# A graph layer on 32 batches: row scales transposed one unit later, VectorE's loop turned at another point of its period, and a new order at the start

## The chip, the cores and the metric

The kernel runs on one core of one Trainium2 chip. The metric is the device time of one execution in microseconds (us); the engines are TensorE (PE), VectorE (DVE), ScalarE (ACT), POOL (GpSimd) and SP (SyncE, which here only issues transfers).

## The reference

The input `x` has 32 batches of 512 channels and 1024 nodes in float32. Per batch:

```
h = relu(layernorm(x over nodes))
q, k = wq.h, wk.h
scores = q[None, :] + k[:, None];  scores = leaky_relu(scores, 0.01)
att = softmax(scores over the last axis)
agg[c, m] = sum_n h[c, n] att[m, n]
out = relu(adj @ agg + bm)
x + out
```

`adj` (512 x 512) serves as the weight matrix of the layer; `wq`, `wk` and `bm` have 512 elements.

## The kernel before

Batches go in pairs, named (i, j) with j 0 or 1; `nxt(b, n)` is the batch n further on, `first` and `second` are (0, 0) and (0, 1). The order of each engine's work is written out by hand, and semaphores tie the engines together. Each float32 operand of a matrix product is split into an upper and a lower float16 part (`h_hi`/`h_lo`, `v_hi`/`v_lo`, `p_hi`/`p_lo`), and three products of parts are summed.

For every batch there are these pieces of work:

- **Normalising.** VectorE takes statistics of `xs` (L633) and computes scale and shift (normaliser). ScalarE writes `h_hi` (L458) and the full `h` in float32 (L464) into one of two buffers; VectorE subtracts them to `h_lo` (h_lower, L687; for the first batch L676).
- **v phase** on TensorE: project_qk (L321) computes q and k, select_qk (L330) brings them into columns after VectorE's copy `qk_rows` (q_rows, L696), spread_qmax (L336) transposes the maximum for VectorE's q_tail. Between them stand eight v_tile of 12 matmuls each (L356 to L358). ScalarE and VectorE split each tile (v_upper L492, v_lower L757).
- **Softmax.** Since the scores are a sum of a row and a column under a leaky relu, the exponential of each is the maximum of two products of a row and a column vector. VectorE sums the rows (denominator, L724, 16 per batch) and turns the sums into row scales `ab_pad` (row_scales, L731 to L735). TensorE transposes `ab_pad` (transpose_ab, L343), VectorE copies the result to `ab_t` (copy_ab, L681), SP writes it to DRAM (L242) and reads it back, spread over the partitions, as `ab_row` (L248).
- **Weights p.** For each of 16 steps per batch ScalarE writes `p_ring` (leak, L480), VectorE takes the maximum (weight, L745), ScalarE writes `p_hi` (L488), VectorE `p_lo` (p_lower, L752). There are two halves of 8 steps; half_0 of a batch is computed one period ahead, the second half in the period itself.
- **Units.** In period b TensorE computes 8 units of 24 matmuls (L379 to L381) from `v` and `p` of b: units 0 to 3 on the first half of p, units 4 to 7 on the second. ScalarE applies the relu (L499), POOL adds `x` (L876), SP stores.

TensorE's period b is: 8 units of b, with transpose_ab(nxt(b)) between them, then the v phase of nxt(b, 2). VectorE's period b is: the second half of the weights of b, between them the denominators of nxt(b); row_scales; h_lower of nxt(b, 2) 0 and 1; copy_ab; h_lower 2 and 3; half_0 of nxt(b); then v_lower, q_head, q_tail, statistics and normaliser of the v phase that TensorE runs meanwhile. The two periods of a pair are the body of a hardware loop: 13 rounds on VectorE and SP, 14 on TensorE, ScalarE and POOL. The periods before and behind are written out.

At the start SP loads the first batch, ScalarE's queue the weights. Absolute sums of the weights give power-of-two scales (scaled_weights on VectorE), POOL scales the weights (L870), TensorE transposes them (L306), and `wmT_hi`/`wmT_lo` come from ScalarE (L450) and VectorE (L622).

Of the kernel before, what the change touches and what calls it, by code (L numbers as in the profile page):

```python
# [43 lines left out]
def gnn_layer(nc, x, adj, wq, wk, bm, out):  # L44
# [14 lines left out]
    with ExitStack() as ctx:  # L59
# [86 lines left out]
        s_su = sem("scaling_chain")  # L146
        s_wqk = sem("wqk_ready")
# [6 lines left out]
        s_h32 = sem("h32_ready")  # L154
        s_hlo = sem("h_split")
# [144 lines left out]
        def _(pe):  # L300
# [44 lines left out]
            def v_tile(b, nt):  # L345
# [55 lines left out]
            pe.wait_ge(s_wqk, 3)  # L401
            project_qk(first)
            select_qk(first)
            spread_qmax(first)
            pe.wait_ge(s_wl, CT)
            for nt in range(NT):
                v_tile(first, nt)
            project_qk(second)
            for nt in range(NT):
# [4 lines left out]
                if nt == 4:  # L414
                    transpose_ab(first)
# [11 lines left out]
        def _(act):  # L427
# [38 lines left out]

            def exponentials(b):
# [27 lines left out]
            def relu(b, k):  # L495
                hf, ot = divmod(k, OT)
                act.wait_ge(s_acc, cnt(b, U, k + 1))
# [51 lines left out]
            h_full(first, 2)  # L549
            weights_upper()  # L550
            h_full(first, 3)
# [31 lines left out]
        def _(dve):  # L583
            def scaled_weights():
                n = [0]

                def link(ins):
                    n[0] += 1
                    ins.then_inc(s_su, 1)
                    dve.wait_ge(s_su, n[0])  # L590

                dve.wait_ge(s_abs, OT + 2)
                dve.wait_ge(s_wv, 16 * 3)

                link(dve.tensor_scalar(rows[:, :], rows[:, :], 1e-25, 1e30, ALU.max, ALU.min))
                link(dve.tensor_scalar(pow2[:, :].bitcast(I32), rows[:, :].bitcast(I32), 0x7F800000, None,
                                       ALU.bitwise_and))
                link(dve.reciprocal(inv2[:, :], pow2[:, :]))
# [3 lines left out]
                dve.tensor_scalar(unscale_o[:, :], pow2[:, 0:OT], 1.0 / (V_BITS * P_SCALE), None,  # L602
                                  ALU.mult).then_inc(s_su, 1)
                dve.tensor_scalar(unscale_q[:, :], pow2[:, OT:OT + 2], 1.0 / (Q_BITS * H_SCALE), None,
                                  ALU.mult).then_inc(s_su, 1)
                n[0] += 4
                dve.wait_ge(s_su, n[0])
                link(dve.memset(wqk[:, :, :], 0.0))
                hi = wqk[:, :, 0:4].rearrange("p t (i s) -> p s i t", s=2)
                link(dve.tensor_copy(hi[:, 0], wqk_col[:, :, :]))  # L610
                dve.tensor_tensor(hi[:, 1], wqk_col[:, :, :], hi[:, 0], ALU.subtract).then_inc(s_wqk, 1)
                dve.wait_ge(s_id, 2)
                pairs = ident[:, :].rearrange("p (g j) -> p g j", g=NQ)[:, :, 0:4].rearrange("p g (i s) -> p s g i", s=2)
                link(dve.tensor_tensor(select[:, :, :], pairs[:, 0], pairs[:, 1], ALU.add))
                for i in range(2):
                    dve.tensor_scalar(select[:, :, i], select[:, :, i], unscale_q[:, i:i + 1], None,
                                      ALU.mult).then_inc(s_wqk, 1)

            def weights_lower():
                for ct in range(CT):  # L620
                    dve.wait_ge(s_wh, ct + 1)
                    dve.tensor_tensor(wmT_lo[:, ct, :], wmT_ps[ct][:, :], wmT_hi[:, ct, :],  # L622
                                      ALU.subtract).then_inc(s_wl, 1)
# [42 lines left out]
            def h_full_first(ct):  # L666
                dve.wait_ge(s_ln, LN_OPS)
                wait(dve, s_hlo, ct - 1)
                dve.tensor_scalar(h32[:, ct % 2, :], xs[:, ct, :], ln_scale[:, 0, ct:ct + 1],
                                  ln_shift[:, 0, ct:ct + 1], ALU.mult, ALU.add).then_inc(s_h32, 1)  # L670

            def h_lower_first(ct):

                dve.wait_ge(s_hhi, ct + 1)
                dve.wait_ge(s_h32, ct + 1)
                dve.scalar_tensor_tensor(out=h_lo[:, 0, ct, :], in0=h32[:, ct % 2, :], scalar=0.0,  # L676
# [91 lines left out]
            def period(b, one, two, three):  # L768
# [45 lines left out]
            for ct in range(CT):  # L814
# [96 lines left out]
```

## Time and profile before

| | before |
|---|---|
| median of 3 runs | 2242.95 us (2241.51 to 2243.74) |
| the profiled execution's own time | 2246.45 us |
| its span | 2244.7 us |
| TensorE busy | 2090.1 us, 93% |
| VectorE busy | 1677.6 us, 75% |
| ScalarE busy | 1225.5 us, 55% |
| POOL busy | 367.9 us, 16% |
| mean granted TensorE clock | 0.973 of full speed |
| DMA | 271.46 MB |

The span is the time from the first to the last instruction of one profiled execution. A wait is idle time of an engine, put down to what released it; "issue" is idle time in which the profile shows nothing that the engine waited for. The starts and ends of matmuls overlap, as they are pipelined: from one start to the next counts.

### The profile page before, as it was taken

How to read it: one execution, taken by the hardware profiler on the slowest of the kernel's cores; microseconds unless marked ns; L12 is line 12 of the kernel's file. 1: busy time of each engine (PE TensorE's matmuls, PEld its weight loads, DVE VectorE, ACT ScalarE, POOL GpSimd, SP SyncE). 2: the span in 40 equal slices, each digit the busy share in tenths (PEclk: the TensorE clock that was granted, in tenths of full speed). 3: DMA queues.
4: the chain of work that ended last, by engine and by line, in shares of the span. 5: the costliest groups of instructions: out<-in, count | busy, mean ns of one | idle time of the engine just before them, and what ended most of it. 6: DMA issues, size and time to landing. Idle time of an engine off the chain costs nothing.

```text
span 2244.7 us, 33555 instructions
## 1 busy us (share of the span) xinstructions
PE 2090.1 (93%) x10448; PEld 956.9 (43%) x10448; DVE 1677.6 (75%) x3667; ACT 1225.5 (55%) x1871; POOL 367.9 (16%) x267
## 2 busy tenths in 40 slices
PE   5899998998989989899898998989989899899999
PEld 2344443443434434444343444434434344344444
DVE  7977787767877678786787767777677777778853
ACT  4655664545645456464565545655456655456634
POOL 0011211111211112111121111211112111122112
PEclk8999999999999999999999999999999999999999
DMA  5134342333323333233442234332343323434222
GB/s 187 70 129 151 132 135 73 125 136 131 141 77 115 136 131 144 83 114 128 136 145 91 102 127 150 131 110 92 122 145 131 127 82 115 145 131 150 89 90 85
DMA packets 126395, 271.46 MB, mean 121 GB/s; under 512 B 22624, under 2 KB 23136, under 8 KB 122208
## 3 DMA queue, kind: packets, MB, share of 16 engines
q1 hardware_dynamic: 123904, 269.01, 34.6%
q10 hardware_dynamic: 2400, 1.58, 0.2%
q14 instruction: 76, 0.62, 0.1%
q8 instruction: 15, 0.25, 0.0%
HBM read 202.91 MB, written 67.63 MB: 121 GB/s over the span
## 4 chain that ended last, share of the span: by engine, by line
PE 56%; DVE 27%; issue 14%; ACT 1%; DMA 1%; DVEq 0%; POOLq 0%; SPq 0%; ACTq 0%
DVE den_out L724 9%; PE mix L379 9%; PE mix L380 9%; PE mix L381 9%; PE mix L356 9%; PE mix L358 8%; PE mix L357 8%; DVE p_ring L745 6%; DVE p_lo L752 5%; PE small L321 1%; DVE den L731 1%; ACT v_hi L492 1%; DVE rstd L659 1%; DVE t_y L658 1%; DVE half_y L656 1%
## 5 line engine op out<-in xcount | busy, mean ns | idle before, releaser
L379 PE MATMUL mix<-p_hi,v_hi 128*128 128x512 f16 x2048 | 789.4, 385 | 5.1 <-DVE p_lo L752 4.4
L380 PE MATMUL mix<-p_lo,v_hi 128*128 128x512 f16 x2048 | 788.1, 385 | 0.0
L381 PE MATMUL mix<-p_hi,v_lo 128*128 128x512 f16 x2048 | 787.2, 384 | 0.0
L876 POOL TENSOR_TENSOR res<-res,y 128x512 f32<-128x512 f32 x256 | 364.3, 1423 | 1856.2 <-ACT y L499 1856.2
L745 DVE SCALAR_TENSOR_TENSOR p_ring<-ab_row,cols,p_ring 128x512 f32<-128x512 f32 x512 | 376.0, 746 | 188.7 <-ACT p_ring L480 131.1
L480 ACT ACTIVATE p_ring<-ab_row,cols 128x512 f32<-128x512 f32 x512 | 349.4, 691 | 166.9 <-DMA ab_row<-ab_rows 106.5
L492 ACT ACTIVATE v_hi<-mix 128x512 f16<-128x512 f32 x256 | 152.7, 597 | 522.6 <-PE mix L358 522.6
L724 DVE SCALAR_TENSOR_TENSOR den_out<-den_row,cols 128x512 f32<-128x512 f32 x512 | 392.4, 802 | 0.0
L356 PE MATMUL mix<-wmT_hi,h_hi 128*128 128x512 f16 x1024 | 389.6, 380 | 0.0
L357 PE MATMUL mix<-wmT_lo,h_hi 128*128 128x512 f16 x1024 | 389.1, 380 | 0.0
L358 PE MATMUL mix<-wmT_hi,h_lo 128*128 128x512 f16 x1024 | 389.1, 380 | 0.0
L757 DVE SCALAR_TENSOR_TENSOR v_lo<-mix,v_hi 128x512 f16<-128x512 f32 x256 | 176.8, 691 | 269.2 <-ACT v_hi L492 266.5
L488 ACT ACTIVATE p_hi<-p_ring 128x512 f16<-128x512 f32 x512 | 302.7, 591 | 124.3 <-DVE p_ring L745 124.3
L752 DVE SCALAR_TENSOR_TENSOR p_lo<-p_ring,p_hi 128x512 f16<-128x512 f32 x512 | 350.3, 684 | 22.5 <-ACT p_hi L488 18.1
L379 PEld LDWEIGHTS mix<-p_hi,v_hi 128*128 128x128 f16 x2048 | 203.1, 99 | 253.4 <-issue 13.9
L381 PEld LDWEIGHTS mix<-p_hi,v_lo 128*128 128x128 f16 x2048 | 203.0, 99 | 249.8 <-issue 14.5
L380 PEld LDWEIGHTS mix<-p_lo,v_hi 128*128 128x128 f16 x2048 | 203.2, 99 | 244.7 <-issue 12.0
L499 ACT ACTIVATE y<-mix,bias_o,unscale_o 128x512 f32<-128x512 f32 x256 | 196.0, 765 | 73.2 <-PE mix L381 73.1
L464 ACT ACTIVATE h<-xs,ln_shift,ln_scale 128x1024 f32<-128x1024 f32 x122 | 147.5, 1232 | 108.8 <-DVE h_lo L687 107.2
L633 DVE BATCH_NORM_STATS2 stats<-xs 128x6 f32<-128x512 f32 x248 | 158.2, 680 | 8.5 <-DMA xs<-in_x_dram 8.5
L356 PEld LDWEIGHTS mix<-wmT_hi,h_hi 128*128 128x128 f16 x1024 | 102.9, 101 | 119.4 <-issue 7.7
L358 PEld LDWEIGHTS mix<-wmT_hi,h_lo 128*128 128x128 f16 x1024 | 100.4, 98 | 121.7 <-issue 1.4
(69 smaller groups left out, 834.1 us busy)
## 6 DMA issues: line engine op xcount, KB each, us to landing
res<-in_x_dram SPq DMA_DIRECT2D x256, 256.0 KB, 2.9
out_dram<-res SPq DMA_DIRECT2D x256, 256.0 KB, 2.1
xs<-in_x_dram SPq DMA_DIRECT2D x124, 512.0 KB, 6.5
den_row<-den_rows SPq DMA_DIRECT2D x32, 1024.0 KB, 4.6
ab_row<-ab_rows SPq DMA_DIRECT2D x64, 512.0 KB, 4.7
res<-in_x_dram SPq DMA_DIRECT2D x4, 512.0 KB, 5.2
wm_nat<-in_adj_dram ACTq DMA_DIRECT2D x1, 1024.0 KB, 12.2
den_rows<-cols SPq DMA_DIRECT2D x32, 8.0 KB, 1.6
```

The costliest lines, as they stand in the source:

```text
L356: pe.matmul(ps[:, :], hi, wmT_hi[:, ct, :], start=(ct == 0), stop=False)
L357: pe.matmul(ps[:, :], hi, wmT_lo[:, ct, :], start=False, stop=False)
L358: mm = pe.matmul(ps[:, :], lo, wmT_hi[:, ct, :], start=False, stop=(ct == CT - 1))
L379: pe.matmul(ps[:, :], v_hi[:, b[1], nt, chans], p_hi[:, hf, nt, :], start=(nt == 0), stop=False)
L380: pe.matmul(ps[:, :], v_hi[:, b[1], nt, chans], p_lo[:, hf, nt, :], start=False, stop=False)
L381: mm = pe.matmul(ps[:, :], v_lo[:, b[1], nt, chans], p_hi[:, hf, nt, :], start=False, stop=(nt == NT - 1))
L480: act.activation(ring[t % RING][:, :], ab_row[:, 1, hf * HALF:(hf + 1) * HALF], ACT.Copy, scale=cols[:, b[1], 1, nt:nt + 1]).then_inc(s_lk, 1)
L488: act.activation(p_hi[:, hf, nt, :], ring[t % RING][:, :], ACT.Copy, scale=P_SCALE).then_inc(s_phi, 1)
L724: dve.scalar_tensor_tensor(out=den_out[:, nodes], in0=den_row[:, 0, nodes], scalar=cols[:, b[1], 2, nt:nt + 1], in1=den_row[:, 1, nodes], ...
L745: dve.scalar_tensor_tensor(out=ring[t % RING][:, :], in0=ab_row[:, 0, hf * HALF:(hf + 1) * HALF], scalar=cols[:, b[1], 0, nt:nt + 1], in1= ...
L752: dve.scalar_tensor_tensor(out=p_lo[:, hf, nt, :], in0=ring[t % RING][:, :], scalar=P_SCALE, in1=p_hi[:, hf, nt, :], op0=ALU.mult, op1=ALU ...
L876: pool.tensor_tensor(res[:, k, :], res[:, k, :], y[:, k % 2, :], ALU.add).then_inc(s_add, 1)
```

## The change

In the steady periods two things change. transpose_ab(nxt(b)) moves on TensorE from unit 4, before its fifth group of three matmuls, to unit 5, before its third group. On VectorE the period is cut into early(b), up to h_lower(h, 3), and late(b), from half_0 on; the loop's body is now late, early, late, early, so that it turns between the last h_lower and half_0, and the first early of the loop is written out ahead of it. The order of VectorE's instructions is the same, and so is the number of rounds.

At the start: the scaling chain is split. POOL clears `wqk` and computes `select`, `unscale_q` and `unscale_o`. The first batch's full `h` of channels 2 and 3 goes into `ab_row` and no longer waits for a buffer of two. VectorE places `scaled_wqk` between the `h_lo` of the first batch, its weights_lower around q_rows, two of the second batch's statistics ahead of q_tail and its normaliser ahead of the `v_lo`. On TensorE spread_qmax(first) stands behind the first v tile, which waits for each `wmT_lo` by itself; the first transpose_ab stands one tile earlier.

```diff
@@ TensorE, v_tile, unit, start @@
                 for ct in range(CT):
+                    if nt == 0 and at(b, first):
+                        pe.wait_ge(s_wl, ct + 1)
...
                 for nt in range(NT):
-                    if one and k == MIX and nt == 4:
+                    if one and k == MIX + 1 and nt == 2:
                         transpose_ab(nxt(b))
...
             transposed_weights()
-            pe.wait_ge(s_wqk, 3)
+            pe.wait_ge(s_wqk, 1)
             project_qk(first)
+            pe.wait_ge(s_sel, 3)
             select_qk(first)
-            spread_qmax(first)
-            pe.wait_ge(s_wl, CT)
             for nt in range(NT):
+                if nt == 1:
+                    spread_qmax(first)
                 v_tile(first, nt)
...
-                if nt == 4:
+                if nt == 3:
                     transpose_ab(first)
@@ ScalarE @@
+            def h_full_first(ct):
+                act.activation(ab_row[:, ct - 2, :], xs[:, ct, :], ACT.Relu, bias=ln_shift[:, 0, ct:ct + 1],
+                               scale=ln_scale[:, 0, ct:ct + 1]).then_inc(s_h32f, 1)
...
-            h_full(first, 2)
+            h_full_first(2)
+            h_full_first(3)
             weights_upper()
-            h_full(first, 3)
             exponentials(first)
@@ VectorE: scaled_weights is split @@
-            def scaled_weights():
...
+            def weight_scales():
...
+            def scaled_wqk():
...
+            def weights_lower(ct):
+                dve.wait_ge(s_wh, ct + 1)
+                dve.tensor_tensor(wmT_lo[:, ct, :], wmT_ps[ct][:, :], wmT_hi[:, ct, :],
+                                  ALU.subtract).then_inc(s_wl, 1)
...
-            def period(b, one, two, three):
+            def early(b, one, two):
                 h = nxt(b, 2)
                 weight(b, NT)
...
                     h_lower(h, 2)
                     h_lower(h, 3)
+
+            def late(b, one, two, three):
+                h = nxt(b, 2)
                 if one:
                     half_0(nxt(b))
...
@@ VectorE, start @@
-            scaled_weights()
-            for ct in range(CT):
-                h_lower_first(ct)
+            weight_scales()
+            h_lower_first(0)
+            h_lower_first(1)
+            scaled_wqk()
+            h_lower_first(2)
+            h_lower_first(3)
+            weights_lower(0)
+            weights_lower(1)
             q_rows(first)
-            weights_lower()
+            weights_lower(2)
+            weights_lower(3)
             q_head(first)
+            statistics(second, 0)
+            statistics(second, 1)
             q_tail(first)
-            for ct in range(CT):
-                statistics(second, ct)
+            statistics(second, 2)
+            statistics(second, 3)
+            normaliser(second)
             v_lower(first, 0)
-            normaliser(second)
             v_lower(first, 1)
+            v_lower(first, 2)
             denominator(first, 0)
-            v_lower(first, 2)
-            denominator(first, 1)
             for ct in range(CT):
                 h_lower(second, ct)
                 v_lower(first, 3 + ct)
-                denominator(first, 2 + ct)
+                denominator(first, 1 + ct)
             v_lower(first, 7)
             q_rows(second)
+            denominator(first, 5)
             denominator(first, 6)
             q_head(second)
             denominator(first, 7)
             row_scales(first)
+            q_tail(second)
             v_lower(second, 0)
-            q_tail(second)
@@ VectorE, the periods @@
-            period((0, 0), True, True, True)
-            period((0, 1), True, True, True)
+            early((0, 0), True, True)
+            late((0, 0), True, True, True)
+            early((0, 1), True, True)
+            late((0, 1), True, True, True)
+            early((1, 0), True, True)
             with dve.Fori(1, PAIRS - 1) as i:
-                period((i, 0), True, True, True)
-                period((i, 1), True, True, True)
+                late((i, 0), True, True, True)
+                early((i, 1), True, True)
+                late((i, 1), True, True, True)
+                early((i + 1, 0), True, True)
...
@@ POOL, start @@
+            pool.memset(wqk[:, :, :], 0.0).then_inc(s_wz, 1)
             pool.memset(ab_pad[:, :], 0.0).then_inc(s_az, 1)
...
+            pool.wait_ge(s_id, 2)
...
+            pool.tensor_scalar(unscale_q[:, :], pow2[:, OT:OT + 2], 1.0 / (Q_BITS * H_SCALE), None,
+                               ALU.mult).then_inc(s_un, 1)
+            pool.tensor_tensor(select[:, :, :], pairs[:, 0], pairs[:, 1], ALU.add).then_inc(s_sel, 1)
+            pool.wait_ge(s_un, 1)
+            pool.wait_ge(s_sel, 1)
+            for i in range(2):
+                pool.tensor_scalar(select[:, :, i], select[:, :, i], unscale_q[:, i:i + 1], None,
+                                   ALU.mult).then_inc(s_sel, 1)
+            pool.tensor_scalar(unscale_o[:, :], pow2[:, 0:OT], 1.0 / (V_BITS * P_SCALE), None,
+                               ALU.mult).then_inc(s_un, 1)
```

VectorE's rows at the end of the loop's body, before (the branch is the turn; the row behind it is the first after the last round):

```order
L662 SCALAR_TENSOR_TENSOR ln_shift<-moments,rstd 128x4
L756 REGISTER_ALU
L757 SCALAR_TENSOR_TENSOR v_lo<-mix,v_hi 128x512
L852 REGISTER_ALU
L852 COMPARE_AND_BRANCH
L745 SCALAR_TENSOR_TENSOR p_ring<-ab_row,cols,p_ring 128x512 x2
```

And with the change:

```order
L691 TENSOR_TENSOR h_lo<-h,h_hi 128x1024
L685 COPY ab_t<-small 16x128
L689 REGISTER_ALU
L691 TENSOR_TENSOR h_lo<-h,h_hi 128x1024
L689 REGISTER_ALU
L691 TENSOR_TENSOR h_lo<-h,h_hi 128x1024
L870 REGISTER_ALU
L870 COMPARE_AND_BRANCH
L749 SCALAR_TENSOR_TENSOR p_ring<-ab_row,cols,p_ring 128x512 x2
L756 SCALAR_TENSOR_TENSOR p_lo<-p_ring,p_hi 128x512
```

The branch stood behind the last `v_lo` of a period; it now stands behind the last two `h_lo`, ahead of the `p_ring` of half_0.

TensorE's rows around the transpose of the row scales in a steady period, before:

```order
L379 MATMUL mix<-p_hi,v_hi 128x512
L380 MATMUL mix<-p_lo,v_hi 128x512
L381 MATMUL mix<-p_hi,v_lo 128x512
L343 MATMUL small<-ident,ab_pad 128x128
L379 MATMUL mix<-p_hi,v_hi 128x512
L380 MATMUL mix<-p_lo,v_hi 128x512
```

And with the change:

```order
L385 MATMUL mix<-p_hi,v_hi 128x512
L386 MATMUL mix<-p_lo,v_hi 128x512
L387 MATMUL mix<-p_hi,v_lo 128x512
L347 MATMUL small<-ident,ab_pad 128x128
L385 MATMUL mix<-p_hi,v_hi 128x512
L386 MATMUL mix<-p_lo,v_hi 128x512
```

In the program the transpose stood at row 323 of TensorE's stream and stands now at row 341: 18 matmuls later.

## Rows read from the trace of the kernel before

**Rows 1.** TensorE's waits over the whole span: engine, tile, line <- who ended it: us in total, times, longest

```profile
PE small L343 <- DVE ab_pad L735: 116.6, 31, 7.0
```

**Rows 2.** TensorE's waits from 350 to 2045 us

```profile
PE small L343 <- DVE ab_pad L735: 103.3, 24, 7.0
```

**Rows 3.** Line 343 by stretches: count, ns min/median/max, first and last start; below, who released it

```profile
L343 PE MATMUL small<-ident,ab_pad x1: 327/327/327, 114.6 to 114.6; 128*128 128x128 f32 x1
  DVE ab_pad L735: 3.9, 1
...
L343 PE MATMUL small<-ident,ab_pad x1: 329/329/329, 249.8 to 249.8; 128*128 128x128 f32 x1
...
L343 PE MATMUL small<-ident,ab_pad x1: 329/329/329, 2180.1 to 2180.1; 128*128 128x128 f32 x1
```

**Rows 4.** Timeline of TensorE: start us, us, engine, line, operation [idle before <- releaser]

```profile
315.70 0.33 PE L343 MATMUL small<-ident,ab_pad 128*128 128x128 f32 x1 [1.86 <-DVE ab_pad L735]
...
386.62 0.47 PE L343 MATMUL small<-ident,ab_pad 128*128 128x128 f32 x1 [6.88 <-DVE ab_pad L735]
...
391.71 0.38 PE L379 MATMUL mix<-p_hi,v_hi 128*128 128x512 f16 x1
...
393.65 0.38 PE L379 MATMUL mix<-p_hi,v_hi 128*128 128x512 f16 x1
```

**Rows 5.** Timeline of VectorE where its loop turns

```profile
363.69 1.42 DVE L745 SCALAR_TENSOR_TENSOR p_ring<-ab_row,cols,p_ring 128x512 f32<-128x512 f32 x2 [4.93 <-issue]
```

**Rows 6.** VectorE's waits over the whole span

```profile
DVE p_ring L745 <- issue: 57.6, 12, 5.0
```

**Rows 7.** The chain that ended last, about 340 and 358 us: start us, us, what

```profile
340.43 0.34 PE small L330 x4
...
358.24 3.06 issue
361.45 2.23 issue
```

**Rows 8.** Stretches: us, busy us of the engines (instructions), granted clock, DMA share, GB/s

```profile
320.00:330.00 10.00, 10.00 (x48) 4.53 (x47) 5.27 (x9) 5.59 (x10) 2.97 (x2) 1.00 0.95 317
...
321.00:331.00 10.00, 10.00 (x48) 4.50 (x47) 5.67 (x9) 6.59 (x12) 2.00 (x2) 1.00 1.02 356
359.00:363.00 4.00, 4.00 (x21) 1.80 (x19) 0.00 (x0) 0.00 (x0) 0.00 (x0) 1.00 0.01 4
...
386.50:391.50 5.00, 4.88 (x13) 1.87 (x14) 4.92 (x6) 2.37 (x2) 0.00 (x0) 0.51 0.29 107
```

**Rows 9.** Timeline of VectorE in an undisturbed period

```profile
313.98 0.68 DVE L752 SCALAR_TENSOR_TENSOR p_lo<-p_ring,p_hi 128x512 f16<-128x512 f32 x1
...
315.47 0.17 DVE L735 TENSOR_TENSOR ab_pad<-cols,ab_pad 128x8 f32<-128x8 f32 x1
...
317.92 0.27 DVE L681 COPY ab_t<-small 16x128 f32<-16x128 f32 x1
...
324.84 1.42 DVE L745 SCALAR_TENSOR_TENSOR p_ring<-ab_row,cols,p_ring 128x512 f32<-128x512 f32 x2 [4.24 <-ACT p_ring L480]
...
335.87 0.41 DVE L696 COPY qk_rows<-small 128x256 f32<-128x256 f32 x1
```

**Rows 10.** Waits of SP, which issues the transfers

```profile
SPq L237 <- DMA den_rows<-cols: 40.4, 32, 4.4
```

**Rows 11.** Timeline of TensorE at the start

```profile
28.76 0.41 PE L321 MATMUL small<-h_hi,wqk 128*32 128x256 f16 x4 [5.58 <-DVE h_lo L676]
...
34.18 0.63 PE L356 MATMUL mix<-wmT_hi,h_hi 128*128 128x512 f16 x1
...
92.36 0.38 PE L379 MATMUL mix<-p_hi,v_hi 128*128 128x512 f16 x1
```

**Rows 12.** Timeline of VectorE at the start

```profile
43.63 0.16 DVE L662 SCALAR_TENSOR_TENSOR ln_shift<-moments,rstd 128x4 f32<-128x4 f32 x1
...
78.30 1.41 DVE L745 SCALAR_TENSOR_TENSOR p_ring<-ab_row,cols,p_ring 128x512 f32<-128x512 f32 x2 [1.11 <-ACT p_ring L480]
```

More of the change, by code:

```diff
@@ L146, in gnn_layer @@
         s_su = sem("scaling_chain")
+        s_wz = sem("wqk_zeroed")
+        s_un = sem("unscales_ready")
+        s_sel = sem("select_ready")
         s_wqk = sem("wqk_ready")
@@ L154, in gnn_layer @@
         s_h32 = sem("h32_ready")
+        s_h32f = sem("first_h32_upper_channels")
         s_hlo = sem("h_split")
@@ L496, in relu @@
                 hf, ot = divmod(k, OT)
+                if k == 0 and at(b, first):
+                    act.wait_ge(s_un, 2)
                 act.wait_ge(s_acc, cnt(b, U, k + 1))
@@ L601, in scaled_weights @@
                                       ALU.mult, ALU.mult).then_inc(s_su, 1)
[L602 to L608, printed above, removed]
+                dve.wait_ge(s_su, 5)
+                dve.wait_ge(s_wz, 1)
                 hi = wqk[:, :, 0:4].rearrange("p t (i s) -> p s i t", s=2)
-                link(dve.tensor_copy(hi[:, 0], wqk_col[:, :, :]))
+                dve.tensor_copy(hi[:, 0], wqk_col[:, :, :]).then_inc(s_su, 1)
+                dve.wait_ge(s_su, 6)
                 dve.tensor_tensor(hi[:, 1], wqk_col[:, :, :], hi[:, 0], ALU.subtract).then_inc(s_wqk, 1)
[L612 to L619, printed above, removed]
-                for ct in range(CT):
-                    dve.wait_ge(s_wh, ct + 1)
-                    dve.tensor_tensor(wmT_lo[:, ct, :], wmT_ps[ct][:, :], wmT_hi[:, ct, :],
-                                      ALU.subtract).then_inc(s_wl, 1)
+            def weights_lower(ct):
+                dve.wait_ge(s_wh, ct + 1)
+                dve.tensor_tensor(wmT_lo[:, ct, :], wmT_ps[ct][:, :], wmT_hi[:, ct, :],
+                                  ALU.subtract).then_inc(s_wl, 1)
             def statistics(b, ct):
@@ L667, in h_full_first @@
                 dve.wait_ge(s_ln, LN_OPS)
-                wait(dve, s_hlo, ct - 1)
-                dve.tensor_scalar(h32[:, ct % 2, :], xs[:, ct, :], ln_scale[:, 0, ct:ct + 1],
-                                  ln_shift[:, 0, ct:ct + 1], ALU.mult, ALU.add).then_inc(s_h32, 1)
+                dve.tensor_scalar(h32[:, ct, :], xs[:, ct, :], ln_scale[:, 0, ct:ct + 1],
+                                  ln_shift[:, 0, ct:ct + 1], ALU.mult, ALU.add).then_inc(s_h32, 2)
             def h_lower_first(ct):
                 dve.wait_ge(s_hhi, ct + 1)
-                dve.wait_ge(s_h32, ct + 1)
-                dve.scalar_tensor_tensor(out=h_lo[:, 0, ct, :], in0=h32[:, ct % 2, :], scalar=0.0,
+                if ct < 2:
+                    src = h32[:, ct, :]
+                    dve.wait_ge(s_h32, 2 * (ct + 1))
+                else:
+                    src = ab_row[:, ct - 2, :]
+                    dve.wait_ge(s_h32f, ct - 1)
+                dve.scalar_tensor_tensor(out=h_lo[:, 0, ct, :], in0=src, scalar=0.0,
                                          in1=h_hi[:, 0, ct, :], op0=ALU.max, op1=ALU.subtract).then_inc(s_hlo, 1)
@@ L849, in _ @@
                     v_lower(second, 4 + nt // 2)
-            period((0, 0), True, True, True)
-            period((0, 1), True, True, True)
-            with dve.Fori(1, PAIRS - 1) as i:
-                period((i, 0), True, True, True)
-                period((i, 1), True, True, True)
-            period((PAIRS - 1, 0), True, True, True)
-            period((PAIRS - 1, 1), True, True, False)
-            period((PAIRS, 0), True, False, False)
-            period((PAIRS, 1), False, False, False)
+            early((0, 0), True, True)
[3 more added lines that the diff above has]
+            early((1, 0), True, True)
+            with dve.Fori(1, PAIRS - 1) as i:
+                late((i, 0), True, True, True)
+                early((i, 1), True, True)
+                late((i, 1), True, True, True)
+                early((i + 1, 0), True, True)
+            late((PAIRS - 1, 0), True, True, True)
+            early((PAIRS - 1, 1), True, True)
+            late((PAIRS - 1, 1), True, True, False)
+            early((PAIRS, 0), True, False)
+            late((PAIRS, 0), True, False, False)
+            early((PAIRS, 1), False, False)
         @block.gpsimd
```

18 lines of the change are left out of this document (8 added, 10 removed).

## The prediction, made before the changed kernel had run

> **What bounds the kernel now.** I read the page first: TensorE is busy 93% of the span and VectorE 75%, so the question is what stands in TensorE's other 7%. The list of TensorE's waits answers it: 116.6 us in 31 waits of one instruction, the small transpose L343 of the row scales, for VectorE's `ab_pad` L735 [rows 1]. Then the single waits. There are two kinds: 1.86 us in an undisturbed period (at 315.70) and 6.88 us after VectorE's loop has turned (at 386.62) [rows 4]. The same list for 350 to 2045 us has 24 of them, 103.3 us [rows 2]: 12 of each kind.
>
> Where the long ones come from, VectorE's timeline shows: an instruction at 363.69 stands after 4.93 us of idleness in which nothing was waited for, "issue" [rows 5]. That happens 12 times, 57.6 us [rows 6], as often as a loop of 13 rounds turns back, between the last `v_lo` of a period and the first `p_ring` of the next. From there VectorE runs without a gap up to `ab_pad` 23 us later, so the whole turn reaches TensorE (6.88 - 1.86 = 5.0).
>
> A second loss follows: after the long wait the granted clock is 0.51 for 5 us, the level of 1.2 GHz, against 1.00 (2.4 GHz) before and after [rows 8]. I price it by periods, from transpose to transpose. The clean one is 249.8 to 315.70 = 65.9, less 1.86 = **64.04 us** of work. From 114.6 to 2180.1 are 30 periods and 2065.5 us [rows 3]; 30 x 64.04 = 1921.2, so 144.3 are lost. The waits in them are 116.6 less the first, 3.9: 112.7. The other **31.6 us** are the clock, mostly 2.4 for each of 12 turns.
>
> **Term 1, the transpose one unit later.** It moves from unit 4, tile 4, to unit 5, tile 2: 18 matmuls of 0.2155 us (9 of them from 391.71 to 393.65 [rows 4]) = 3.88 us later. In the undisturbed period TensorE was ready at 315.70 − 1.86 = 313.84, so now at 317.72; `ab_pad` is done at 315.64 [rows 4, 9]. The wait is gone with 2.1 us to spare. What is late next? The unit's last tile needs the last `p_lo`, done at 314.66 (313.98 + 0.68); TensorE reaches it 9 matmuls after 313.84, at 315.78: 1.1 us to spare. Behind the transpose VectorE copies its result at 317.92, after two `h_lo`; now the result is there at 317.72 + 0.33 = 318.05, so the copy, the two row DMAs of SP queued behind it and the first `p_ring` slip by some 0.2 us. VectorE idles 4.24 us before that `p_ring` [rows 9], and TensorE needs those weights only a v phase later. By itself this move would take the 12 long waits from 6.9 to 3 or 4.
>
> **Term 2, the turn of VectorE's loop moved** from the end of the v phase to between the last `h_lo` of early() and half_0. The row beside it is the gap of 4.24 us before `p_ring` at 324.84, a wait for ScalarE, which waits for the row DMAs. The gap begins at 320.60; plus 4.93 is 325.53, so the turn makes half_0 0.7 us late, with the copy 0.9. TensorE's first need of VectorE behind it is L330, which needs `qk_rows`, done at 335.87 + 0.41 = 336.28; L330 ran at 340.43, and with the 1.9 us that TensorE gains at 338.57 [rows 7, 9]. So VectorE may be 2.3 us late, and is 0.9: 1.4 us of cover. With that cover gone TensorE would stand at L330, and behind it the v phase. VectorE has short waits before its `v_lo` there, in which it catches up. Every wait of TensorE for `ab_pad` goes: 116.6, less what the first period keeps.
>
> The trace has no turn at the new place, so its length is bounded: below, 4.93 us less what VectorE's sequencer may run ahead (no loss at all); above, by the transfers. At the old place the DMA engines carry 4 GB/s during the turn at a share of 0.01 and nothing else; from 321 to 331 us, the new place, they are at 1.02 with 356 GB/s [rows 8]. Small transfers wait under load: the one before L237 takes 40.4 / 32 = 1.3 us, at worst 4.4 [rows 10]. The chain shows the turn in two pieces, 3.06 and 2.23 us [rows 7]. If each is a transfer of code, the turn grows by at most 2 × 3.1 = 6.2 us. The Trainium skill ("Runtime: NRT & Kernel Launch", section "Instruction fetch mechanics") speaks for that reading: a taken branch to code outside the window held forces a DMA fetch before the engine goes on. By that rule the turn is a transfer and suffers from the load (up to 58 us more in all); by the idle row alone it stays 4.93 and costs nothing. The trace agrees as far as the 4 GB/s go; no row shows a fetch under load. Between 0 and (6.2 − 1.4) × 12 = 58 us I take 0.3 per turn, **3.6 us**, near the lower end, since the branch can be reached while the last `h_lo` (1.2 us) still runs, and the burst only begins with it.
>
> **Term 3, the clock.** With no wait left it has no idleness to fall after: in 320 to 330 TensorE is busy 10.00 of 10 us at 1.00 [rows 8]. The 31.6 us come back.
>
> **Term 4, the start.** The first projection (28.76) waits 5.58 us for `h_lo` [rows 11], because ScalarE's third `h` waits for a buffer and the fourth comes after the weights. Now both follow the `h_hi` directly, in `ab_row`: `h_lo` ends about 25.1, 3.5 us earlier, and v_tile 0 starts near 28.6 instead of 34.18 [rows 11], as the spread of the maximum moves behind it. But the spread then comes 12 slow matmuls later at about 33.7, as before (it ran just ahead of 34.18): `q_tail`, the exponentials and the row DMAs don't move. What moves is the second batch's normaliser: two of its four statistics now stand ahead of `q_tail`, and a `v_lo` behind it, so it ends at about 40.5 instead of 43.8 [rows 12], 3.3 earlier. Behind it VectorE works nearly without gaps up to the copy of the scales, and the row DMAs follow that; so the first `p_ring` comes at about 75.1 instead of 78.30 [rows 12]. Unit 0 of the first batch is tied to `p_lo`, so it ends **3.2 us** earlier. The scaling chain's parts now on POOL (some 10 small operations, memset included) hide behind the projection, as `select` is wanted only near 27.6.
>
> In the first period the wait of 3.9 becomes one for the last `p_lo`: from the start of unit 1 (92.36 [rows 11]) TensorE needs 93 × 0.2155 = 20.0, at 112.4; it is done one us before `ab_pad` (the transpose is at 114.6 [rows 3]), at 113.5. So 1.1 stays and 115.5 of the 116.6 go.
>
> **Sum.** 115.5 + 31.6 + 3.2 − 3.6 = 146.7. The profiled execution took 2246.45 (span 2244.7, 1.75 around it), so 2099.75. The median of the three runs, 2242.95, is 3.5 lower: **2096.3 us**.
>
> **The rivals.**
> *The turn grows under the DMA load* (above). For: share 1.02 at the new place. Against: the branch can be reached while `h_lo` still runs. One piece delayed by 3.1: (3.1 − 1.4) × 12 = 20, **2113**; both by 3.1, with the clock falling again (2.4 each): 58 + 29 − 4, **2179**.
> *VectorE's p_lo takes the place of the scales.* Cover 1.1 us. If VectorE runs 2 us later against TensorE, 0.9 × 28 = 25: **2121**. Against it: the 22.9 us from `v_lo` to `ab_pad` hold nothing that the change touches.
> *The turn does not go under the gap* but adds to it (the engine sees the wait only after the turn, and the copy, row loads and turn lie in series): 4.9 late, (4.9 + 0.2 − 2.3) × 12 = 34 − 4: **2127**. Then the change does only its first half.
> *Slower than before*, one mechanism: each of the two pieces of a turn waits for the burst of transfers, 10 us long from 321 on. Gain lost = 12 × (growth − 1.4 + 2.4); it is 150 us, the whole gain, at a growth of 11.5 us. At 15 the time is 2092.7 + 192 = **2285**. For: nothing but the share above 1. Against: small transfers grew by 3.1 at most.
>
> **How the numbers follow.** Forecast 0.70; the turn grown 0.15, p_lo 0.05, in series 0.06, slower 0.02, anything else on the fast side 0.02. About 0.2% (4.5 us) is what a measurement here can tell from no change; only the slower rival and its neighbourhood come near. Faster 0.97, same 0.01, slower 0.02. Range: below, the turn costs nothing (2092.7) and the start gives twice its 3.2 and more, 2087; above, it takes in the first rival's first half, the second and third, 2135.
>
> **What would show it.** Right: L343's successor waits for nothing; the 12 "issue" gaps stand before the first `p_ring` of half_0 with the wait for ScalarE smaller there, or are partly hidden; periods of 64.0 us throughout; granted clock 1.00 from 120 us on. Wrong: a wait of L330's successor for `qk_rows` in every second period; gaps above 6.3 us at the turn; waits for `p_lo` in unit 4; a first `p_ring` not before 77 us.

## The result and the profile after

The changed kernel takes **2089.64 us** (median of 4 runs, 2088.49 to 2090.47), the kernel before beside it 2242.39 us (2241.51 to 2243.74): a ratio of 0.9318, 95% interval 0.9302 to 0.9334, so 6.8% or 152.8 us less. I had forecast 2096.3 with a range from 2087 to 2135. The profiled execution took 2090.47 us, its span is 2088.7.

The page of the changed kernel, its busy times, the granted clock by slices, and the chain that ended last by engine:

```profile
PE 2051.5 (98%) x10448; PEld 950.3 (45%) x10448; DVE 1674.8 (80%) x3661; ACT 1221.5 (58%) x1871; POOL 379.6 (18%) x273
...
PEclk9999999999999999999999999999999999999999
...
PE 95%; DVE 3%; DMA 1%; POOL 0%; issue 0%; ACT 0%; POOLq 0%; SPq 0%; DVEq 0%
```

TensorE is busy 98% of the span instead of 93%, and the chain lies on it for 95%; before, the same line read PE 56%, DVE 27%, issue 14%. TensorE's waits, the view of [rows 1]:

```profile
PE mix L310 <- POOL wm_nat L893: 23.2, 2, 21.9
PE mix L385 <- DVE p_lo L756: 5.4, 8, 1.1
PE small L325 <- DVE h_lo L691: 2.8, 1, 2.8
PE small L334 <- DVE qk_rows L700: 0.6, 1, 0.6
PE mix L385 <- DVE v_lo L761: 0.5, 1, 0.5
```

The row of 116.6 us is gone and nothing of its size stands in its place; all that is left lies ahead of 112 us. The transposes, now L347, one by one, as in [rows 3]:

```profile
L347 PE MATMUL small<-ident,ab_pad x1: 272/272/272, 176.9 to 176.9; 128*128 128x128 f32 x1
...
L347 PE MATMUL small<-ident,ab_pad x1: 272/272/272, 240.7 to 240.7; 128*128 128x128 f32 x1
...
L347 PE MATMUL small<-ident,ab_pad x1: 272/272/272, 304.6 to 304.6; 128*128 128x128 f32 x1
...
L347 PE MATMUL small<-ident,ab_pad x1: 273/273/273, 368.4 to 368.4; 128*128 128x128 f32 x1
...
L347 PE MATMUL small<-ident,ab_pad x1: 272/272/272, 2028.0 to 2028.0; 128*128 128x128 f32 x1
```

Every period is 63.83 us long ((2028.0 - 176.9) / 29), with a turn of VectorE's loop in it (304.6 to 368.4 and every second one after) or without. The clock, by stretches (the columns of [rows 8]):

```profile
119.00:2080.00 1961.00, 1961.00 (x9995) 908.44 (x9994) 1574.86 (x3422) 1156.91 (x1774) 360.47 (x250) 1.00 0.38 130
```

From 119 to 2080 us TensorE is busy throughout, and the granted clock is 1.00, the upper level.

Where did the turn go? VectorE's timeline in a period in which the loop turns, behind the last `h_lo`, and what it waits for over the whole span (its row "issue" of [rows 6] doesn't exist any more):

```profile
366.33 0.17 DVE L739 TENSOR_TENSOR ab_pad<-cols,ab_pad 128x8 f32<-128x8 f32 x1
366.50 2.36 DVE L691 TENSOR_TENSOR h_lo<-h,h_hi 128x1024 f16<-128x1024 f32 x2
368.78 0.27 DVE L685 COPY ab_t<-small 16x128 f32<-16x128 f32 x1
369.11 2.36 DVE L691 TENSOR_TENSOR h_lo<-h,h_hi 128x1024 f16<-128x1024 f32 x2
375.44 1.41 DVE L749 SCALAR_TENSOR_TENSOR p_ring<-ab_row,cols,p_ring 128x512 f32<-128x512 f32 x2 [3.97 <-ACT p_ring L491]
...
386.40 0.41 DVE L700 COPY qk_rows<-small 128x256 f32<-128x256 f32 x1
```

```profile
DVE p_ring L749 <- ACT p_ring L491: 129.7, 33, 7.0
```

The first `p_ring` comes 3.97 us after `h_lo`, released by ScalarE. In the 27 periods between the fifth and the last the gap is 3.7 to 4.3 us, in those with a turn no longer than in the others. The turn lies wholly under a wait that was there anyway; how long it is there, the gap doesn't tell (see "How long a turn is"). It costs nothing, and the copy isn't late either: the transpose ends at 368.68, the copy starts at 368.78. TensorE's L334 ran at 389.04, 2.2 us behind `qk_rows`.

### The profile page after: what moved, and what is told of

Read it like the earlier page. It is cut to its first block, busy times and chain, and to the rows that moved or that the text cites. A ratio compares the mean times of both kernels' runs of the same rounds, so it can differ in the third digit from the quotient of the medians.

```text
span 2088.7 us, 33534 instructions
## 1 busy us (share of the span) xinstructions
PE 2051.5 (98%) x10448; PEld 950.3 (45%) x10448; DVE 1674.8 (80%) x3661; ACT 1221.5 (58%) x1871; POOL 379.6 (18%) x273
## 4 chain that ended last, share of the span: by engine, by line
PE 95%; DVE 3%; DMA 1%; POOL 0%; issue 0%; ACT 0%; POOLq 0%; SPq 0%; DVEq 0%
PE mix L385 21%; PE mix L387 21%; PE mix L386 21%; PE mix L362 10%; PE mix L363 10%; PE mix L364 10%; PE small L325 2%; DVE den_out L728 1%; PE small L334 1%; DMA xs<-in_x_dram 0%; DVE p_ring L749 0%; DVE p_lo L756 0%; DVE v_lo L761 0%; POOL wm_nat L893 0%; DMA den_row<-den_rows 0%
## 5 line engine op out<-in xcount | busy, mean ns | idle before, releaser
L385 PE MATMUL mix<-p_hi,v_hi 128*128 128x512 f16 x2048 | 776.3, 379 | 5.9 <-DVE p_lo L756 5.4
L386 PE MATMUL mix<-p_lo,v_hi 128*128 128x512 f16 x2048 | 776.2, 379 | 0.0
L387 PE MATMUL mix<-p_hi,v_lo 128*128 128x512 f16 x2048 | 776.2, 379 | 0.0
L911 POOL TENSOR_TENSOR res<-res,y 128x512 f32<-128x512 f32 x256 | 370.5, 1447 | 1688.2 <-ACT y L512 1688.2
```

The source lines that it names most:

```text
L385: pe.matmul(ps[:, :], v_hi[:, b[1], nt, chans], p_hi[:, hf, nt, :], start=(nt == 0), stop=False)
L386: pe.matmul(ps[:, :], v_hi[:, b[1], nt, chans], p_lo[:, hf, nt, :], start=False, stop=False)
L387: mm = pe.matmul(ps[:, :], v_lo[:, b[1], nt, chans], p_hi[:, hf, nt, :], start=False, stop=(nt == NT - 1))
L911: pool.tensor_tensor(res[:, k, :], res[:, k, :], y[:, k % 2, :], ALU.add).then_inc(s_add, 1)
```

## The experiments

All ratios are against the kernel before, run on the same chip beside each.

### Four kernels that take the change apart

The transpose alone, on the kernel before:

```diff
-                    if one and k == MIX and nt == 4:
+                    if one and k == MIX + 1 and nt == 2:
                         transpose_ab(nxt(b))
```

> The kernel before with the transpose moved from unit 4 to unit 5 and nothing else. My sum: the 16 short waits (1.86 us) go, 30 us; the 12 waits behind a turn shrink from 6.9 to what is left for the last p_lo, 5.0 - 1.1 = 3.9 us, 36 us. If the clock still falls after 3.9 us of waiting, as it did once at 114.5, the result is 2242.4 - 66 = 2176; if it does not, 29 us more, 2147. The rival, that the move gives nearly all (the turn would then never have reached TensorE through anything but the transpose), says 2100 or less.

Measured: **2158.6 us**, 0.9624 (0.9608 to 0.9640). The turn alone, on the kernel before:

```diff
             with dve.Fori(1, PAIRS - 1) as i:
-                period((i, 0), True, True, True)
-                period((i, 1), True, True, True)
+                late((i, 0), True, True, True)
+                early((i, 1), True, True)
+                late((i, 1), True, True, True)
+                early((i + 1, 0), True, True)
```

> The kernel before with VectorE's loop cut between the last h_lo and half_0 and nothing else. My sum: 12 long waits become short ones, 12 x 5.0 = 60 us, and the clock's loss behind them goes, up to 29 us: 2242.4 - 60 = 2182 if waits of 1.9 us also let the clock fall, 2153 if they don't. 28 waits of 1.86 us for ab_pad stay. The rival (the turn lies in series with the wait for the row loads, or grows under their load) says 2190 to 2240, with idle time of VectorE marked issue or a longer wait before p_ring.

Measured: **2158.91 us**, 0.9623 (0.9607 to 0.9639). Both of these diffs together, with the start of the kernel before:

> Both steady moves with the start of before. My sum leaves the start 3.2 us: 2089.6 + 3.2 = 2093. If the start is worth more (as the time below my forecast would allow), up to 2096; if nothing, 2090. No wait for ab_pad behind the first period.

Measured: **2091.94 us**, 0.9325 (0.9309 to 0.9340). And the changed kernel with both undone, that is with its start alone:

> The start of the change with the steady periods of before. By my sum 2242.4 - 3.2 = 2239. If the start helps only where TensorE waits for nothing else later, the waits for ab_pad eat none of it, since all later work moves with it: the same 2239. Nothing gained would be 2242.

Measured: **2242.58 us**, 1.0002 (0.9992 to 1.0012), no difference.

Either half of the steady change is worth 85 us, and both together 152, 18 less than the sum of 170. So they are mostly two debts, but not wholly: the wait behind a turn, 6.75 us on average, is shortened by either, by 4.9 us with the turn moved and by 3.3 with the transpose moved, which is 1.4 us more than there is to take, 12 times. Their traces say which is which. TensorE's largest wait with the transpose alone:

```profile
PE mix L379 <- DVE p_lo L752: 47.2, 32, 2.6
```

and with the turn alone:

```profile
PE small L343 <- DVE ab_pad L735: 58.0, 30, 3.9
```

With the transpose alone the 16 short waits are gone, and the 12 turns have moved to the last two `p_lo` of unit 4: 47.2 less the 5.4 of the start are 3.5 for each turn, where I had 3.9. The clock lies between my two cases: a period with a turn is 69.3 us and one without 63.8, so 2.0 us beside the wait. Part of that is the clock: behind the second wait, from 372.14 us on, matmuls stand 0.43 us apart for 3 us instead of 0.2155, which is 1.5 of the 2.0. With the turn alone the periods are 65.9 us throughout, that is 63.83 + 1.86 + 0.2: the short waits stay, and after them the clock does not fall here:

```profile
379.40:384.40 5.00, 5.00 (x24) 2.34 (x25) 4.78 (x5) 3.04 (x3) 0.75 (x1) 1.00 0.35 113
```

So the expectation for the turn alone (2153, clock kept) is met but for 6 us, the 0.2 us of 30 periods that the wait row doesn't contain.

The start alone is a miss, and an instructive one. In its trace the wait for `ab_pad` is 103.4 us instead of 116.6, and yet the 30 periods from 109.6 to 2174.5 us take 2064.9 us, where the kernel before needs 2065.5 from 114.6 to 2180.1. So 13 us less of waiting gained these periods 0.6 us; the rest went into the clock. After a short wait, in the kernel before and then in this one:

```profile
594.50:599.50 5.00, 5.00 (x25) 2.29 (x25) 4.71 (x5) 3.04 (x3) 0.82 (x1) 1.00 0.32 114
```

```profile
584.90:589.90 5.00, 5.00 (x16) 1.97 (x17) 4.82 (x5) 2.79 (x3) 0.00 (x0) 0.66 0.32 108
```

The first stays at 1.00 after its 1.9 us, the second falls after its 2.1; here that happens after 9 of 13 such waits, while in the kernel before it happened once, after a wait of 1.90 at 182.2 us. That the length of the wait decides is likely by this, not shown. And where did the 13 us less waiting come from? Not from the start, but from the turn, which has another shape:

```profile
354.89 1.41 DVE L749 SCALAR_TENSOR_TENSOR p_ring<-ab_row,cols,p_ring 128x512 f32<-128x512 f32 x2 [2.54 <-issue]
...
357.10 0.75 DVE L728 SCALAR_TENSOR_TENSOR den_out<-den_row,cols 128x512 f32<-128x512 f32 x1 [0.80 <-issue]
```

It takes 2.54 + 0.80 us where the kernel before has 4.93 in one piece [rows 5], at the same place of the period. In the loop nothing but its position in VectorE's stream differs, by a few instructions. That called for a test of its own.

### How long a turn is

Here 64, 128 and 192 waits on a semaphore that is long reached are put at VectorE's very start in the kernel before. Nothing else changes.

```diff
+            for _ in range(64):
+                dve.wait_ge(s_id, 1)
             for ct in range(CT):
                 statistics(first, ct)
```

> The kernel before with 64 more waits on a long reached semaphore at VectorE's very start, where it idles for the first load anyway; they only push the loop 64 instructions down VectorE's stream. In the start-only kernel, whose loop stands a few instructions higher, the turn took 2.5 us before the first p_ring and 0.9 before the first den_out instead of 4.8 in one. If the turn is a reload of code in blocks, its length and where it is felt depend on where the loop stands to the blocks: another split or length here, between 0 and 5 us, and the wait for ab_pad follows it one to one. If the difference had another cause (what runs beside it), the turn stays 4.8 us and the time 2243.6.

> As p64 with 128 waits. Reload in blocks: again another split or length. Otherwise 4.8 us and 2243.6.

> As p64 with 192 waits. Reload in blocks: again another split or length; with 64, 128 and 192 at least one of the three differs from 4.8 us by over 1 us. Otherwise 4.8 us in all three and 2243.6.

Measured: **2214.61** (0.9870, 0.9842 to 0.9899), **2215.96** (0.9876, 0.9848 to 0.9905) and **2237.7 us** (0.9976, 0.9965 to 0.9987). The program grows by 32, 64 and 96 instructions by the page, as two waits go into one. VectorE's turns, for 64, 128 and 192:

```profile
DVE p_ring L745 <- issue: 31.1, 12, 2.7
```

```profile
DVE p_ring L745 <- issue: 30.1, 12, 2.8
```

```profile
DVE p_ring L745 <- issue: 29.8, 12, 2.7
```

2.5 to 2.6 us each instead of 4.8, in all three. And the trace shows the reloads themselves: one DMA queue carries packets marked "instruction", 8 KB each. Its row (packets, MB, share of 16 engines) over one turn, from 358.5 to 363.7 us in the kernel before and from 356.7 to 359.1 with 64 waits:

```profile
q14 instruction: 2, 0.02, 1.0%
```

```profile
q14 instruction: 1, 0.01, 1.2%
```

It is so in every turn: two packets, 2.4 to 2.9 us apart, in each of the 12 turns of the kernel before and one in each of the 36 of the padded kernels. In the start-only kernel one lies in the first gap and the next begins at 355.3, 1.0 us ahead of the second. So the reading of the turn as a reload of code in blocks holds: the kernel before stood where it took two reloads, and a few dozen instructions further one is enough. The Trainium skill ("Runtime: NRT & Kernel Launch", section "Instruction fetch mechanics") states the rule for a taken branch to code outside the held window; the 2.5 and 4.8 us are this case's, and no run shows where the blocks' borders lie. That the 192 waits gain only 6.5 us, where the others gain 28 to 30, goes with what was just met: the same turn, but short waits of 2.1 us instead of 1.9 and a granted clock of 0.973 over the span, against 0.988 and 0.983. Why the short wait is 0.2 us longer there, no run shows.

The same row settles how long the turn is in the changed kernel. Over 371.0 to 375.5 us, the gap with the turn in it:

```profile
q14 instruction: 1, 0.01, 1.3%
```

The packet begins at 371.4, as the last `h_lo` ends, and the next one follows at 375.8, behind the `p_ring`; in the other turns the two are 3.6 us apart or more, where the kernel before had 2.4 to 2.9. So the moved turn took one reload and not the two that its 4.93 us stood for. The 2.5 us that one reload takes without load would fit into the gap of 4.24; whether the load that sets in there made it longer, the gap hides.

The other half of the question is what the load at the new place does to a turn. This kernel is the changed one with the loop turned in the middle of half_0, where VectorE has no gap and the transfers run:

```diff
-            def half_0(b):
-                weight(b, 0)
-                for nt in range(NT):
+            def half_0(b, steps):
+                if steps[0] == 0:
+                    weight(b, 0)
+                for nt in steps:
...
+                if one:
+                    half_0(nxt(b), range(4))
+
             def late(b, one, two, three):
                 h = nxt(b, 2)
                 if one:
-                    half_0(nxt(b))
+                    half_0(nxt(b), range(4, NT))
```

> The changed kernel with VectorE's loop turned in the middle of half_0, between its steps 3 and 4, where VectorE has no gap and the DMA engines are loaded. This bares the length of a turn under load. If it stays 4.9 us, qk_rows is 4.9 us late against 2.2 us of cover (386.81 to 389.04), 2.7 x 12 = 32 us: 2122, or 2151 with the clock falling each time. If each of its two pieces takes 3.1 us longer, 8.9 x 12 = 107 us: 2197 to 2225. The trace shows the idle time as issue.

Measured: **2108.0 us** (2100.94 to 2113.34), 0.9386 (0.9371 to 0.9400). One turn, the load around it (share 1.01, 408 GB/s), and the sums for VectorE and TensorE:

```profile
383.93 0.76 DVE L749 SCALAR_TENSOR_TENSOR p_ring<-ab_row,cols,p_ring 128x512 f32<-128x512 f32 x1 [2.91 <-issue]
...
513.59 0.76 DVE L749 SCALAR_TENSOR_TENSOR p_ring<-ab_row,cols,p_ring 128x512 f32<-128x512 f32 x1 [4.23 <-issue]
```

```profile
379.00:381.00 2.00, 2.00 (x11) 0.92 (x10) 2.00 (x4) 2.00 (x4) 0.00 (x0) 1.00 1.01 408
```

```profile
DVE p_ring L749 <- issue: 44.2, 12, 4.9
```

```profile
PE small L334 <- DVE qk_rows L700: 15.7, 13, 2.3
```

Turns under load last from 2.9 to 4.9 us, 3.7 on average, and they scatter, which the runs do too (12 us between the fastest and the slowest). Each of the 12 has one instruction packet in its gap, so the load adds 0.4 to 2.4 us to the 2.5 of one reload. It adds them before the packet: that begins 0.8 to 2.9 us after VectorE falls idle, 0.4 to 0.7 in the padded kernels. A turn of two reloads under load was not run; the rival of the prediction, growth to 11 us or more, had no sign of itself here. The price is near the sum: 3.7 less 2.2 of cover is 1.5 for a turn, 18 us, and by the medians 18.4 were measured. That the two are so close is luck: the turns are those of the profiled execution, which was the slowest of the four, 22.9 us above the change's, and in it the clock fell three times.

### Where the transpose may stand

Further back, in unit 6:

```diff
-                    if one and k == MIX + 1 and nt == 2:
+                    if one and k == MIX + 2 and nt == 2:
```

> The changed kernel with the transpose 24 matmuls later still, in unit 6. It is 5.2 us later, VectorE's copy waits 5.1 us for it, and with it the row loads and half_0. Against 2.2 us of cover before select_qk this costs 2.9 us in each of 31 periods: 90 us, 2180, and up to 2.4 us more in each if the clock falls, 2254. The rival, that the cover is larger because the row loads then fall into a quieter stretch or VectorE catches up, says 2090 to 2130.

Measured: **2273.1 us**, 1.0134 (1.0119 to 1.0150), slower than before the change. No wait for `ab_pad` is left here, and yet:

```profile
394.68 0.28 DVE L685 COPY ab_t<-small 16x128 f32<-16x128 f32 x1 [5.03 <-PE small L347]
```

```profile
PE small L334 <- DVE qk_rows L700: 101.9, 31, 3.7
```

```profile
413.00:418.00 5.00, 4.67 (x16) 2.06 (x17) 1.87 (x6) 0.86 (x2) 1.27 (x1) 0.66 0.53 170
```

VectorE waits 5.03 us for the transpose, the rows come as much later, and TensorE stands 3.3 us before L334 in every period (2.9 expected), after which the clock falls to 0.66 over 5 us. That makes periods of 69 to 71 us, where the kernel before has 65.9 without a turn. The mechanism is as worked out, but the time lies 19 us above the dearest of my cases (2254): a period costs 5.9 us more than in the change, of which 3.3 are the wait, where I had 2.9, and 2.6 what follows it, where I had 2.4 at most.

Less far back, in unit 4 before its last three matmuls:

```diff
-                    if one and k == MIX + 1 and nt == 2:
+                    if one and k == MIX and nt == 7:
```

> The changed kernel with the transpose only 9 matmuls later than before (unit 4, before the last three matmuls). TensorE would reach it 1.94 us later than before, where the short wait was 1.86: the wait is gone by 0.1 us and the time is 2090. If a wait remains (0 to 0.4 us, since waits of a few hundred ns cost the pipeline more than themselves), 2090 + 31 x 0.2 to 0.5 = 2096 to 2105.

Measured: **2097.43 us**, 0.9352 (0.9337 to 0.9366), 7.8 us more than the change, 0.25 for each of 31 periods. The second case: the list of waits shows none, but the transpose starts 0.48 us after the matmul ahead of it instead of 0.22, and lasts 0.33 us instead of 0.27.

```profile
301.68 0.38 PE L387 MATMUL mix<-p_hi,v_lo 128*128 128x512 f16 x1
302.16 0.33 PE L347 MATMUL small<-ident,ab_pad 128*128 128x128 f32 x1
302.33 0.38 PE L385 MATMUL mix<-p_hi,v_hi 128*128 128x512 f16 x1
```

### The start

In the changed kernel POOL's scaling of the weights takes 6.91 us, where it took 2.78, and TensorE's first transposes end the later for it:

```profile
18.96 2.36 DVE L680 SCALAR_TENSOR_TENSOR h_lo<-h,h_hi 128x1024 f16<-128x1024 f32 x2
19.03 6.91 POOL L893 TENSOR_SCALAR wm_nat<-wm_nat,inv 128x512 f32<-128x512 f32 x4 [17.37 <-DVE inv L605]
...
25.99 1.11 PE L310 MATMUL mix<-ident,wm_nat 128*128 128x128 f32 x4 [1.25 <-POOL wm_nat L893]
...
27.04 0.40 PE L325 MATMUL small<-h_hi,wqk 128*32 128x256 f16 x4
```

This kernel puts scaled_wqk back ahead of `h_lo`:

```diff
+            scaled_wqk()
             h_lower_first(0)
             h_lower_first(1)
-            scaled_wqk()
             h_lower_first(2)
```

> The changed kernel with the scaled wqk ahead of the first two h_lo on VectorE, as the kernel before had it. In the changed kernel POOL's four weight scalings took 6.91 us beside h_lo instead of 2.78 us beside small operations. If VectorE's h_lo slows POOL, the scalings shorten to about 4 to 5 us here, as only their first part runs beside small operations, the first projection comes about 1 us earlier, and the time is 2089 (same within the noise or 1 us less). If POOL's time has another cause it stays 6.9 us.

Measured: **2090.37 us**, 0.9316 (0.9303 to 0.9329), no difference, and POOL's sum stays at 6.90 us, against what I expected. But the single scalings moved with `h_lo`. The rows of line 893 by stretches (count, ns min/median/max, first and last start), the change first:

```profile
L893 POOL TENSOR_SCALAR wm_nat<-wm_nat,inv x1: 2772/2772/2772, 19.0 to 19.0; 128x512 f32<-128x512 f32 x1
...
L893 POOL TENSOR_SCALAR wm_nat<-wm_nat,inv x1: 2787/2787/2787, 23.1 to 23.1; 128x512 f32<-128x512 f32 x1
```

```profile
L893 POOL TENSOR_SCALAR wm_nat<-wm_nat,inv x1: 777/777/777, 19.0 to 19.0; 128x512 f32<-128x512 f32 x1
...
L893 POOL TENSOR_SCALAR wm_nat<-wm_nat,inv x1: 2789/2789/2789, 20.4 to 20.4; 128x512 f32<-128x512 f32 x1
...
L893 POOL TENSOR_SCALAR wm_nat<-wm_nat,inv x1: 2704/2704/2704, 23.2 to 23.2; 128x512 f32<-128x512 f32 x1
```

A scaling lasts 0.7 us, or 2.7 to 2.8 us if it begins beside a pair of `h_lo` (at 18.96 and 23.11 in the change, at 20.36 and 22.63 here), about until the pair is done. Each of the two kernels has two such meetings, so the sum is the same. That the one engine holds up the other is shown by that; what they share is not.

The last kernel takes up idle time of VectorE at the start:

```diff
+            statistics(second, 2)
             q_tail(first)
-            statistics(second, 2)
             statistics(second, 3)
...
+            h_lower(second, 0)
             denominator(first, 0)
             for ct in range(CT):
-                h_lower(second, ct)
+                if ct > 0:
+                    h_lower(second, ct)
```

> The changed kernel with a third statistic of the second batch ahead of q_tail, where VectorE idles 1.85 us, and the second batch's first h_lo ahead of the first denominators, which wait 0.97 us for their rows. If VectorE's own work sets the start up to the first p_ring, as my sum had it, that comes about 1.1 us earlier and the time is 2088.5. If the rows' transfers set it, nothing moves: 2089.6. A h_lo that has to wait for ScalarE would cost up to 1 us: 2090.5.

Measured: **2088.59 us** (2088.06 to 2089.72), 0.9310 (0.9297 to 0.9323). In the profiled executions the first `p_ring` of the steady work moved from 75.81 to 73.89 us, and the span from 2088.7 to 2086.8, 1.9 us less where I had 1.1. The change's first `p_ring`, this one's, and that of the start-only kernel, whose start is the change's:

```profile
75.81 1.42 DVE L749 SCALAR_TENSOR_TENSOR p_ring<-ab_row,cols,p_ring 128x512 f32<-128x512 f32 x2 [0.76 <-ACT p_ring L491]
```

```profile
73.89 1.42 DVE L749 SCALAR_TENSOR_TENSOR p_ring<-ab_row,cols,p_ring 128x512 f32<-128x512 f32 x2 [0.45 <-ACT p_ring L491]
```

```profile
73.34 1.41 DVE L749 SCALAR_TENSOR_TENSOR p_ring<-ab_row,cols,p_ring 128x512 f32<-128x512 f32 x2
```

The third row takes the meaning from the first two: with the start of the change left as it is, the first `p_ring` comes anywhere from 72.27 (the kernel of unit 6) to 75.81 us in the traces here, so 73.89 need not come from this edit. The medians differ by 1.05 us and the intervals of the ratios overlap. Whether the edit gains its microsecond is open.

## Why the prediction was right, point by point

- **What bounds the kernel.** Right: the only row of size was the wait for `ab_pad`, and with it gone TensorE idles nowhere between 119 and 2080 us.
- **Term 1, the transpose one unit later.** Right in mechanism and size. `ab_pad` is ready 1.9 us ahead of the transpose (366.50 to 368.41; I had 2.1), the copy isn't late, the last `p_lo` comes in time. The transpose alone shows the next limit where I had named it, at `p_lo`, with 3.5 us for my 3.9.
- **Term 2, the turn.** Right: it lies under the wait for the row loads, and its packet begins as the last `h_lo` ends, ahead of most of the burst, as I had argued. I allowed 3.6 us for it, and it cost nothing. Two things in its working were not as I had them. The turn was taken as 4.93 us wherever it stands; the padded kernels show that this was an accident of position, and at the new place the turn has one reload, not two. That was luck, as I had not placed it so; my 0.9 us of lateness against 2.3 us of cover was never put to the test. And the load did not make a turn grow to 11 us; where it is bare, it scatters between 2.9 and 4.9, again with one reload. The cover of 2.3 us before L330 was 2.2.
- **Term 3, the clock.** Right for the whole: the clock is at 1.00, and the loss is gone. What I took for work was too long: 64.04 us, a period of 65.9 less its wait of 1.86, still holds 0.2 us that a wait costs TensorE beyond its row (I call it the restart). The period without a wait is 63.83 us, and 30 x 0.21 = **6.3 us** came back beside the 31.6; it is the largest item by which the sum fell short.
- **Term 4, the start.** Mis-sized: I had 3.2 us, and the comparison of the change with its halves on the old start gives 2091.94 - 2089.64 = 2.3 us by the medians. The profiled executions of before and after say 2.5 (TensorE's last wait for `p_lo` in unit 0 ends at 89.23 instead of 91.70), while those of the halves and of the change are only 0.9 apart, and first `p_ring` rows that differ by up to 3.5 us under the same start say how little one trace settles here. The first projection came at 27.04 instead of the 25.2 of my sum, as POOL's scalings took 6.91 us; I had written that POOL's work hides behind the projection and had not asked what VectorE's `h_lo` does to it. That this is what the start lacks is not shown. The first period went as I had it: the wait for `p_lo` at 111.13 is 1.01 us, and no other comes after 90 us.
- **The sum.** For the profiled execution I had 2099.75 and it took 2090.47, 9.3 us less: 6.3 from the restarts and 3.6 from the turn make 9.9, and the start with the first period gave 0.6 less than I had: from the transpose at 114.6, which now is 3.88 us of work further on, to 113.1 are 5.4 us, where my sum has 3.2 + 2.8. The medians are 6.7 us apart, since the profiled execution of before lay 3.5 us above its median and that of after 0.8.
- **The rivals.** The grown turn did not show in the change, where it could have grown only unseen under the gap; `p_lo` in the place of the scales showed only with the turn left where it was, and turn and gap in series did not happen. The slower rival has a cousin that is real: with the transpose a unit further back the kernel is 1.3% slower than before the change, by the same cover of 2.2 us before select_qk.

## What to carry to other kernels

Where an engine in the chain has a gap that another wait makes anyway, a loop's turn is free there; look for it before shortening anything. A transpose or a copy that hands work between engines has a slot with two ends: too early one engine waits, too late the other, and here 3.9 us further was right while 9.1 us was worse than the old place. Work out both covers from the timeline before choosing.

And before a small gain or loss is put down to an edit, see whether the edit moved a loop in the instruction stream: 32 instructions more made the kernel before 1.3% faster, and 96 more only 0.2%. The DMA queue marked "instruction" shows how many reloads a turn takes.

## What the runs showed that I had not expected

- A turn of VectorE's loop, with no transfers beside it, took 4.8 us or 2.5 us, or 2.5 and 0.8 in two pieces, by the loop's position in the stream: with two 8 KB instruction packets in the gap, with one, or with one ahead of each piece. The loops of TensorE and ScalarE showed no such gap in any profile here.
- The granted clock falls to the lower level not only after waits of 5 to 7 us, but sometimes after one of 2.1 us (0.66 over the next 5 us), while after waits of 1.9 us it mostly stayed at 1.00. Twelve turns shorter by 1.5 us gained nothing in the start-only kernel, whose clock fell after 9 of its 13 short waits.
- A wait costs TensorE some 0.2 us beyond its row: periods of 65.9 us with a wait of 1.86 against 63.83 without.
- One of POOL's 128x512 scalings lasts 0.7 us, or 2.8 us when it begins beside two back-to-back `h_lo` of VectorE.
